# Turning the context of a Perceiver block by transposing DMAs instead of TensorE

## The chip, the cores and the metric

The kernel runs on one core of one Trainium2 chip, as one program. The metric is the device time of one execution in microseconds (us), the median of several runs. A profiled execution has the same kind of time, and beside it a span: from the first instruction of the core to the last.

## What is computed

Two batches (b = 0, 1) of 256 query tokens with 256 features attend to a context of 4096 tokens with 256 features; a second attention (hyperbolic distance) and a mixture of experts follow. Only the first attention and its inputs matter here:

```python
def xattn(query, key, value, w_q, w_k, w_v, w_o):     # 16 heads of 64
    q = (query @ w_q).reshape(B, Q, 16, 64).transpose(0, 2, 1, 3)
    k = (key @ w_k).reshape(B, 4096, 16, 64).transpose(0, 2, 1, 3)
    v = (value @ w_v).reshape(B, 4096, 16, 64).transpose(0, 2, 1, 3)
    attn = softmax(einsum('bhqd,bhkd->bhqk', q, k) * 64 ** -0.5)
    out = einsum('bhqk,bhkd->bhqd', attn, v)
    return out.transpose(0, 2, 1, 3).reshape(B, Q, 1024) @ w_o
x = x + xattn(layernorm(x), ctx, ctx, w_q, w_k, w_v, w_o)    # ctx: (2, 4096, 256) float32
x = x + attn(layernorm(x), ...)
x = x + ffn(layernorm(x), ...)
```

## The kernel before

**Steps and periods.** The first attention runs in 16 steps (STEPS), each for one pair of heads (hp) and one batch; ORDER lists them. A step has eight periods (q = 0 to 7), one for each chunk of 512 keys. In one period TensorE (PE) takes for the present step the shifts (L1431) and scores (L1443) of 512 keys, projects the values of the chunk (project_v, L1359) and multiplies the probabilities of the period before with values (L1486 to L1491). Beside that it computes for the next step the score blocks whose maximum is wanted (maxima, L1390) and projects the keys of the step after a chunk ahead (project_k, L1330). ScalarE (ACT) takes exponentials (L1677), high parts of probabilities (L1686), values and keys (L1643, L1637). VectorE (DVE) reduces the maxima (L1849), takes the high part of every fourth slot (split_p, L1877) and the low parts of values and keys (L1870, L1840). GpSimd (POOL) takes the low parts of the probabilities (L2048). Everything is in program order on each engine, with semaphores between them.

**High and low parts.** Each float32 factor is carried as two float16 arrays: the high part is the value cast, the low part is the value less the high part. A product takes three matmuls: high by high, high by low, low by high.

**The context.** Features must lie on the partitions for the projections, so each chunk of 512 tokens x 256 features is turned. `ctx_hi` and `ctx_lo` hold the turned parts of both batches. The raw chunks of batch 0 are loaded to `probs` and to the half of `k_p` that step 1 uses; those of batch 1 lie in the place of its own turned parts, one chunk further on.

**The stretch before step 0.** For i = 0 to 9 (the eight chunks of batch 0 and EARLY = 2 of batch 1) transposes_ctx(i) turns a chunk with eight float32 transposes on PE (L1288). ACT's context(i) reads the result from PSUM twice, once for the high part (L1660) and once for a float32 copy (L1662), for GpSimd cannot read PSUM. GpSimd subtracts the two for the low part (L2026). The next chunk's transposes wait for the second read, for they use the same two banks. Beside this PE projects the keys of step 0 (project_first_k, L1346), ACT and DVE take their high and low parts (L1637, L1840), and maxima of step 0 go through PE and DVE. At the end come the queries of step 1, its first chunk of keys, the greatest of the maxima (take_max) and the turned rows of it (max_rows); then step 0 begins.

**The rest of batch 1.** Step 1 was of batch 1, so its six other chunks (LATER_AT) are turned in the periods 0 to 5 of step 0: eight transposes on PE in two halves (transposes_later), two reads of 512 columns by ACT (L1667) and two by DVE (L1864).

**The queues.** All DMAs are issued from SyncE's queue (SP): x, the weights of steps 0 and 1, eight loads of batch 0, sixteen half chunks of batch 1, and then the weights for each step after its waits.

Of the kernel before, what the change touches and what calls it, by code (L numbers as in the profile page):

```python
# [59 lines left out]
TURNED = 2  # L60
EARLY = 2
PERIODS = SLOTS // 4
PAIRS_A_STEP = SLOTS // 2
LATER_AT = {q: q + EARLY for q in range(KCH - EARLY)}
# [37 lines left out]
def perceiver(nc, x, ctx, wq, wk, wv, wo, aq, ak, av, ao, gw, gb, w1, b1, w2, b2, out):  # L102
# [8 lines left out]
    with stack:  # L111

        ps = stack.enter_context(nc.psum_tensor("ps", [P, 8, 512], FP32))
        ctx_hi = sb("ctx_hi", [P, B, NC, TK], FP16)
        ctx_lo = sb("ctx_lo", [P, B, NC, TK], FP16)
# [6 lines left out]
        level = sb("level", [P, P], FP16)  # L122
        spare = sb("spare", [P, TK * 2])
# [34 lines left out]
        raw1 = [m[:, 1, :, :].rearrange("p c k -> p (c k)").bitcast(FP32)  # L158
                .rearrange("p (c u d) -> p c u d", c=NC, d=D) for m in (ctx_hi, ctx_lo)]
# [7 lines left out]
        copies = psums[:, :, :, :, :].rearrange("p b k h q -> p b k (h q)")  # L167


        hi32 = ctx_hi[:, :, :, :].rearrange("p b c k -> p (b c k)").bitcast(FP32)  # L170
        lo32 = ctx_lo[:, :, :, :].rearrange("p b c k -> p (b c k)").bitcast(FP32)
# [75 lines left out]
        s_tp = sem("s_tp")  # L247
        s_th = sem("s_th")
        s_tl = sem("s_tl")
        s_cx = sem("s_cx")  # L250
        s_ch = sem("s_ch")
        s_cl = sem("s_cl")
# [89 lines left out]
        def context_part(i):  # L342

            b, u = divmod(i, KCH)
            return b, u, slice(512 * u, 512 * (u + 1))

        def raw_tile(b, u, t):

            if b == 0:
                n = u // 2  # L350
                return stage[n // 2][:, n % 2, 4 * (u % 2) + t, :]
            if u == KCH - 1:
                return last_raw[:, t, :]
            return raw1[t // 2][:, t % 2, u + 1, :]
# [860 lines left out]
        def _(sp):  # L1215
# [18 lines left out]
            for u in range(KCH):  # L1234
                tiles = slice(4 * (u % 2), 4 * (u % 2) + 4)
                sp.dma_start(stage[u // 4][:, u // 2 % 2, tiles, :], chunks[0, u // 2, :, tiles, :]) \
                    .then_inc(s_ctx[u], 16)
                if u == 2:
                    load_wv(0, 0)
                    load_wqk(1, 0)  # L1240
            for u in range(KCH):
                for i in range(2):
                    to = last_raw[:, 2 * i:2 * i + 2, :] if u == KCH - 1 else raw1[i][:, :, u + 1, :]
                    first = 4 * (u % 2) + 2 * i
                    sp.dma_start(to, chunks[1, u // 2, :, first:first + 2, :]).then_inc(s_raw[u], 16)
            def load_experts(w):
                sp.dma_start(w_raw.rearrange("p (m n) -> p m n", n=F),
                             w.rearrange("e (c p) n -> p (e c) n", p=P)).then_inc(s_ew, 16)
# [22 lines left out]
            for n in range(STEPS):  # L1271
                step(n)
            tail_sp(sp)
# [3 lines left out]
        def _(pe):  # L1277
# [7 lines left out]

            def turn_context(b, u, c, bank):
                for t in range(CS):
                    mm = pe.transpose(ps[:, bank, t * P:(t + 1) * P],  # L1288
                                      raw_tile(b, u, t)[:, c * P:(c + 1) * P], ident[:, :])
                return mm  # L1290

            def transposes_ctx(i):

                b, u, _ = context_part(i)
                if b == 0:
                    pe.wait_ge(s_ctx[u], 16)
                else:
                    pe.wait_ge(s_raw[u], 32)
                at_least(pe, s_th, i)
                for c in range(NC):  # L1300
                    mm = turn_context(b, u, c, TURNED + c)
                mm.then_inc(s_tp, 1)

            def transposes_later(q, u, c):

                if c == 0:
                    pe.wait_ge(s_raw[u], 32)
                else:
                    pe.wait_ge(s_vl, q + 1)
                turn_context(1, u, c, (SIDE, PV)[c]).then_inc(s_cx, 1)  # L1310
# [10 lines left out]
            def project_k(j, n, par, b, bank):  # L1321
# [3 lines left out]
                if n == 1 and j >= EARLY:  # L1325
                    pe.wait_ge(s_cl, 2 * (j - EARLY) + 2)
                keys = slice(512 * j, 512 * (j + 1))
                for c in range(NC):
                    for i, (w, y) in enumerate(((wk_hi, ctx_hi), (wk_hi, ctx_lo), (wk_lo, ctx_hi))):
                        mm = pe.matmul(ps[:, bank, :], w[:, par, c, :], y[:, b, c, keys],  # L1330
                                       start=(c == 0 and i == 0), stop=(c == 1 and i == 2))
                mm.then_inc(s_k, 1)

            def project_first_k(j, bank):

                if j == 0:
                    pe.wait_ge(s_wkl, 1)
                keys = slice(512 * j, 512 * (j + 1))
                products = [(w, y, c) for w, y in ((wk_hi, ctx_hi), (wk_lo, ctx_hi), (wk_hi, ctx_lo))
                            for c in range(NC)]  # L1340
                for i, (w, y, c) in enumerate(products):
                    if i == 0:
                        pe.wait_ge(s_th, j + 1)
                    if i == 4:
                        pe.wait_ge(s_tl, j + 1)
                    mm = pe.matmul(ps[:, bank, :], w[:, 0, c, :], y[:, 0, c, keys],  # L1346
                                   start=(i == 0), stop=(i == 5))
                mm.then_inc(s_k, 1)

            def project_v(j, n, par, b, bank, halves=(0, 1)):  # L1350
# [3 lines left out]
                for t in [2 * half + i for half in halves for i in range(2)]:  # L1354
                    toks = slice((CS * j + t) * P, (CS * j + t + 1) * P)
                    k = 0
                    for c in range(NC):
                        for y, w in ((ctx_hi, wv_hi), (ctx_hi, wv_lo), (ctx_lo, wv_hi)):
                            mm = pe.matmul(ps[:, bank, t * P:(t + 1) * P], y[:, b, c, toks],  # L1359
# [5 lines left out]
            def maxima(u, n, par):  # L1365
# [13 lines left out]
                if n == 1 and t == 0:  # L1379
                    at_least(pe, s_cl, min(2 * j - 1, NC * len(LATER_AT)))  # L1380
# [74 lines left out]
            def values_bank_free(n, q):  # L1455
# [4 lines left out]
                if n == 0 and q - 1 in LATER_AT:  # L1460
                    pe.wait_ge(s_cl, 2 * q)
# [40 lines left out]
            def step(n):  # L1502
                par, b, first = n % 2, ORDER[n][1], n == 0
                for q in range(PERIODS):
# [18 lines left out]
                    if first and q in LATER_AT:  # L1523
                        transposes_later(q, LATER_AT[q], 0)
# [10 lines left out]
                    if first and q in LATER_AT:  # L1535
                        transposes_later(q, LATER_AT[q], 1)
# [49 lines left out]
            transposes_ctx(0)  # L1586
            transposes_x()
            project_first_k(0, PV)
            transposes_ctx(1)
            pe.wait_ge(s_xc, NC)  # L1590
            project_q(0, 0, 0)
            for j in range(2, KCH + 2):
                transposes_ctx(j)
                if j < KCH + 1:
                    at_least(pe, s_kl, j - 2)
                    project_first_k(j - 1, (PV, PK)[(j - 1) % 2])
                else:
                    pe.wait_ge(s_kl, KCH - 1)
                    project_q(1, 1, 1)
                maxima(2 * (j - 2), 0, 0)  # L1600
                maxima(2 * (j - 2) + 1, 0, 0)
            pe.wait_ge(s_kl, KCH)
            pe.wait_ge(s_tl, KCH + 1)
            project_k(0, 1, 1, 1, PK)
            max_rows(0)
            pe.wait_ge(s_tl, KCH + EARLY)
            pe.wait_ge(s_const, 4)
# [473 lines left out]
```

## Time and profile before

| | |
|---|---|
| median of 3 runs | 1123.02 us (1120.26 to 1123.82) |
| the profiled execution | 1124.97 us |
| its span | 1123.3 us |
| mean granted TensorE clock | 0.971 |
| step 0 begins (us from the span's start) | 50.3 |
| busy: PE, PEld, DVE, ACT, POOL | 94%, 70%, 72%, 71%, 61% |

PE is the matmul side of TensorE, PEld its weight loads. The profiled execution took 1.95 us more than the median of the three runs. A busy share is a mean over stretches with different limits, so each stretch has to be read by itself.

### The profile page before, as it was taken

What the parts mean: (1) busy time and instruction counts of PE and PEld (TensorE: products, weight loads), DVE (VectorE), ACT (ScalarE), POOL (GpSimd) and SP (SyncE); (2) the same over time, 40 slices, a digit from 0 to 9 for tenths busy, and PEclk for the clock granted to TensorE, in tenths of its full rate; (3) what the DMA queues carried; (4) which work ended last, traced back from release to release, by engine and by line L of the source; (5) the groups of instructions that cost most, each with busy time, mean ns of one, the idle gap of its engine ahead of it and who ended that gap; (6) DMA issues with size and microseconds to landing.
All of it is one profiled execution on the core that took longest, in us unless ns stands there. A gap on an engine that the chain in (4) does not pass through costs nothing.

```text
span 1123.3 us, 36747 instructions
## 1 busy us (share of the span) xinstructions
PE 1051.4 (94%) x15493; PEld 789.3 (70%) x15493; DVE 810.9 (72%) x1059; ACT 796.4 (71%) x1452; POOL 680.1 (61%) x614
## 2 busy tenths in 40 slices
PE   5899999999999999999999999999999999666688
PEld 3477777777777777777777777777777777543466
DVE  3887777777777777777777777777767759457442
ACT  4776776777777777777777777777776756798854
POOL 3665666666666666666666666676665556734233
PEclk9999999999999999999999999999999999787799
DMA  9100000000000000000000000003000010000000
GB/s 329 51 2 16 7 17 7 17 6 17 7 16 7 17 7 17 7 16 8 17 7 16 8 16 7 16 8 119 7 2 7 28 52 3 2 1 1 1 1 20
DMA packets 27381, 25.45 MB, mean 23 GB/s; under 512 B 1850, under 2 KB 25938, under 8 KB 27218
## 3 DMA queue, kind: packets, MB, share of 16 engines
q1 hardware_dynamic: 27218, 23.10, 6.5%
q8 instruction: 124, 2.03, 0.7%
q14 instruction: 39, 0.32, 0.1%
HBM read 22.57 MB, written 0.52 MB: 21 GB/s over the span
## 4 chain that ended last, share of the span: by engine, by line
PE 81%; DVE 8%; issue 4%; ACT 4%; POOL 2%; DMA 1%; SPq 0%; ACTq 0%; POOLq 0%; DVEq 0%
PE ps L1359 15%; PE ps L1330 14%; PE ps L1443 13%; PE ps L1390 6%; PE ps L1491 5%; PE ps L1486 5%; PE ps L1489 5%; PE ps L1431 4%; PE ps L759 2%; PE ps L719 2%; POOL psums L2048 2%; PE ps L1422 1%; PE ps L1316 1%; DVE m_part L1849 1%; PE ps L535 1%
## 5 line engine op out<-in xcount | busy, mean ns | idle before, releaser
L2048 POOL TENSOR_TENSOR psums<-probs 128x512 f16<-128x512 f32 x512 | 590.1, 1172 | 317.5 <-ACT probs L1686 264.2
L1677 ACT ACTIVATE probs<-ps 128x512 f32<-128x512 f32 x512 | 279.7, 600 | 199.2 <-PE ps L1443 198.3
L1849 DVE TENSOR_REDUCE m_part<-ps 128x2 f32<-128x1024 f32 x256 | 313.2, 1224 | 142.8 <-PE ps L1390 142.7
L1686 ACT ACTIVATE probs<-probs 128x512 f16<-128x512 f32 x384 | 242.1, 632 | 0.3
L1443 PE MATMUL ps<-q_hi,k_p 64*128 64x256 f16 x2048 | 211.1, 269 | 0.0
L1486 PE MATMUL ps<-v_sb,probs 128*128 128x65 f16 x2048 | 205.9, 193 | 4.5 <-POOL psums L2048 4.5
L1489 PE MATMUL ps<-v_sb,probs 128*128 128x64 f16 x2048 | 205.8, 192 | 0.0
L1491 PE MATMUL ps<-v_sb,psums 128*128 128x65 f16 x2048 | 205.4, 194 | 0.0
L1486 PEld LDWEIGHTS ps<-v_sb,probs 128*128 128x128 f16 x2048 | 188.4, 98 | 19.0 <-POOL psums L2048 6.1
L1489 PEld LDWEIGHTS ps<-v_sb,probs 128*128 128x128 f16 x2048 | 188.0, 97 | 15.6
L1491 PEld LDWEIGHTS ps<-v_sb,psums 128*128 128x128 f16 x2048 | 188.2, 97 | 0.0
L1359 PE MATMUL ps<-wv_hi,ctx_hi 128*128 128x128 f16 x1024 | 180.5, 221 | 1.6 <-DVE v_sb L1870 1.6
L1359 PE MATMUL ps<-wv_lo,ctx_hi 128*128 128x128 f16 x1024 | 179.2, 220 | 0.0
L1359 PE MATMUL ps<-wv_hi,ctx_lo 128*128 128x128 f16 x1024 | 179.2, 220 | 0.0
L1877 DVE CAST probs<-probs 128x512 f16<-128x512 f32 x128 | 147.7, 1154 | 1.6 <-ACT probs L1677 1.4
L1443 PE MATMUL ps<-q_lo,k_p 64*128 64x256 f16 x1024 | 142.8, 269 | 0.0
L1359 PEld LDWEIGHTS ps<-wv_hi,ctx_hi 128*128 128x128 f16 x1024 | 100.2, 98 | 40.2 <-issue 38.3
L1443 PEld LDWEIGHTS ps<-q_hi,k_p 64*128 64x128 f16 x2048 | 106.1, 94 | 19.5
L1840 DVE TENSOR_TENSOR k_p<-ps,k_p 128x512 f16<-128x512 f32 x128 | 88.5, 691 | 33.3 <-ACT k_p L1637 33.3
L1390 PE MATMUL ps<-k_p,q_hi 64*128 64x512 f16 x512 | 99.0, 380 | 13.2 <-DVE m_part L1849 7.9
L1359 PEld LDWEIGHTS ps<-wv_lo,ctx_hi 128*128 128x128 f16 x1024 | 100.6, 98 | 0.1
L1359 PEld LDWEIGHTS ps<-wv_hi,ctx_lo 128*128 128x128 f16 x1024 | 100.4, 98 | 0.0
(246 smaller groups left out, 1704.4 us busy)
## 6 DMA issues: line engine op xcount, KB each, us to landing
ctx_hi<-in_L_ffn_W_dram SPq DMA_DIRECT2D x2, 2048.0 KB, 9.7
wqk_raw<-in_L_xattn_w_q_dram SPq DMA_DIRECT2D x16, 128.0 KB, 2.3
wqk_raw<-in_L_xattn_w_k_dram SPq DMA_DIRECT2D x16, 128.0 KB, 2.5
probs<-in_ctx_dram SPq DMA_DIRECT2D x4, 512.0 KB, 7.4
wv_raw<-in_L_xattn_w_v_dram SPq DMA_DIRECT2D x16, 128.0 KB, 2.5
k_p<-in_ctx_dram SPq DMA_DIRECT2D x4, 512.0 KB, 9.2
wo_raw<-in_L_xattn_w_o_dram SPq DMA_DIRECT2D x16, 128.0 KB, 2.1
ctx_hi<-in_ctx_dram SPq DMA_DIRECT2D x7, 256.0 KB, 7.0
```

Of the source, the lines that this page charges most:

```text
L1330: mm = pe.matmul(ps[:, bank, :], w[:, par, c, :], y[:, b, c, keys], start=(c == 0 and i == 0), stop=(c == 1 and i == 2))
L1359: mm = pe.matmul(ps[:, bank, t * P:(t + 1) * P], y[:, b, c, toks], w[:, par, c, :], start=(k == 0), stop=(k == 5))
L1390: mm = pe.matmul(ps[:, bank + 1 - h, :], q_hi[rows, n % 3, t * P:(t + 1) * P], k_p[rows, par, 0, 512 * j:512 * (j + 1)], start=True, stop= ...
L1443: mm = pe.matmul(ps[:, score_bank(n, pair, h), cols], k_p[rows, par, k_part, keys], q_part[rows, n % 3, :], start=False, stop=(i == 2), sk ...
L1486: pe.matmul(out, p_hi[:, s % NP, h, queries], value[:, XD:2 * XD + 1], start=(s == 0 and h == 0 and t == 0), stop=False, skip_group_check= ...
L1489: pe.matmul(ps[:, ACC, at:at + XD], p_hi[:, s % NP, h, queries], value[:, 0:XD], start=False, stop=False, skip_group_check=True)
L1491: mm = pe.matmul(out, p_lo[:, s % NP, h, queries], value[:, XD:2 * XD + 1], start=False, stop=(s == SLOTS - 1), skip_group_check=True)
L1677: nc.scalar.activation(p_raw[:, s:s + 2, h, :], ps[:, score_bank(n, pair, h), :].rearrange("p (k q) -> p k q", k=2), ACT.Exp, scale=XSCALE ...
L1686: nc.scalar.activation(p_hi[:, s % NP, :, :], p_raw[:, s % NX, :, :], ACT.Copy) \
L1849: nc.vector.tensor_reduce(m_part[:, j, t, :], ps[:, bank:bank + 2, :], AX.X, ALU.max) \
L1877: nc.vector.tensor_copy(p_hi[:, s % NP, :, :].rearrange("p h q -> p (h q)"), p_raw[:, s % NX, :, :].rearrange("p h q -> p (h q)")) \
L2048: nc.gpsimd.tensor_tensor(p_lo[:, s % NP, :, :].rearrange("p h q -> p (h q)"), p_raw[:, s % NX, :, :].rearrange("p h q -> p (h q)"), p_hi[ ...
```

## The change

1. The raw chunks are split where they lie, tokens on the partitions: ACT casts 128x1024 for the high part (split_context_high) and GpSimd takes raw less high for the low part (split_context_low), both into `nat`, a ring of NAT = 8 buffers. No PE transposes, no copies through PSUM.
2. Each part is turned by a transposing DMA of 128x1024 float16 (256 KB) within SBUF, from the SP queue (turn_context). A chunk needs two. `ctx_hi` and `ctx_lo` are laid out by chunk.
3. Batch 0 is now loaded from ACT's queue, batch 1 from SP's between the turning DMAs.
4. For the keys of step 0, the low part is made in PSUM: a further matmul adds minus the identity times the high part (subtract_high), and ACT casts what is left (take_low_k). DVE's subtraction of before is gone there. ACT casts up to LEAD = 4 chunks ahead.
5. Steps 0 and 1 are both of batch 0 (head pairs 0 and 1), so batch 1 is first needed by step 2's keys (FIRST1 = 2), from period 7 of step 0. Its chunks 2 to 7 are split in halves of 128x512, one in each of the first twelve periods: on ACT ahead of the period's exponentials, on DVE between the two maxima.
6. GpSimd's constants for the tail come at the beginning and not after the chunks.

```diff
-ORDER = tuple((i // 2, i % 2) for i in range(STEPS - 6)) + tuple(
+ORDER = ((0, 0), (1, 0), (0, 1), (1, 1)) + tuple((i // 2, i % 2) for i in range(4, STEPS - 6)) + tuple(
     (hp, b) for b in range(B) for hp in range(HP - 3, HP))
+FIRST1 = 2
-TURNED = 2
-LATER_AT = {q: q + EARLY for q in range(KCH - EARLY)}
+SPLIT_AT = {g: (KCH + EARLY + g // 2, g % 2) for g in range(2 * (KCH - EARLY))}
+NAT = 8
+LEAD = 4
+        def split_context_high(act, i, halves=(0, 1)):
+            b, u = divmod(i, KCH)
+            if b == 0:
+                act.wait_ge(s_ctx[u], 16)
+            else:
+                act.wait_ge(s_raw[u], 32)
+            if i >= NAT:
+                act.wait_ge(s_dh[i % NAT], 16)
+            parts = raw_parts(i)
+            for raw, tiles in [parts[h] for h in halves if h < len(parts)]:
+                last = nc.scalar.activation(nat_part(i, 0, tiles), raw, ACT.Copy)
...
+        def split_context_low(eng, ops, i, halves=(0, 1)):
...
+            for raw, tiles in [parts[h] for h in halves if h < len(parts)]:
+                last = ops.tensor_tensor(nat_part(i, 1, tiles), raw, nat_part(i, 0, tiles), ALU.subtract)
...
+            def turn_context(i, low):
...
+                sp.dma_start((ctx_hi, ctx_lo)[low][:, b, u, :, :].rearrange("p c (t k) -> p (c t) k", t=CS),
+                             nat[:, i % NAT, low, :], transpose=True).then_inc((s_dh, s_dl)[low][i % NAT], 16)
+            turn_context(0, 0)
+            for u in range(1, KCH + 1):
+                if u < KCH:
+                    turn_context(u, 0)
+                turn_context(u - 1, 1)
+                if u - 1 in (3, 5):
+                    load_context((u - 4) // 2)
+            for u in range(2, KCH):
+                load_context(u)
+                if u in (3, 5):
+                    turn_context(KCH + u // 4, 0)
+                    turn_context(KCH + u // 4, 1)
...
             for n in range(STEPS):
+                if n == 2:
+                    for u in range(EARLY, KCH - 3):
+                        turn_context(KCH + u, 0)
+                        turn_context(KCH + u, 1)
                 step(n)
+                if n == 2:
+                    for u in range(KCH - 3, KCH):
+                        turn_context(KCH + u, 0)
+                        turn_context(KCH + u, 1)
...
             pe.wait_ge(s_const, 3)
-            transposes_ctx(0)
             transposes_x()
-            project_first_k(0, PV)
-            transposes_ctx(1)
+            project_first_k(0, 0)
             pe.wait_ge(s_xc, NC)
             project_q(0, 0, 0)
-            for j in range(2, KCH + 2):
-                transposes_ctx(j)
...
+            project_first_k(0, 1)
+            pe.wait_ge(s_const, 5)
+            for j in range(KCH):
+                if j + 1 < KCH:
+                    for part in range(2):
+                        project_first_k(j + 1, part)
+                subtract_high(j)
+                maxima(2 * j, 0, 0)
+                maxima(2 * j + 1, 0, 0)
...
             split_k(0, 0)
-            context(0)
+            split_context_high(act, 0)
+            split_context_high(act, 1)
...
+            split_context_high(act, 2)
             take_q(0)
+            split_context_high(act, 3)
+            for j in range(KCH):
+                take_k(j, 0, 0, (PV, PK)[j % 2])
+                if j >= 1:
+                    take_low_k(j - 1)
+                if j + LEAD < KCH:
+                    split_context_high(act, j + LEAD)
```

## Rows read from the trace of the kernel before

**Rows 1.** The chain that ended last, to period 5 of step 0: start us, us, what.
```profile
2.34 6.08 DMA probs<-in_ctx_dram
...
26.18 1.04 PE ps L1288 x8
27.24 1.02 ACT ctx_hi L1660
28.26 0.93 ACT psums L1662
...
42.38 0.61 PE ps L1346 x2
...
80.56 0.66 PE ps L1443 x12
...
88.00 0.66 PE ps L1443 x12
```
**Rows 2.** TensorE's timeline: first and fifteenth maxima of step 0, first instruction of step 0.
```profile
22.25 0.61 PE L1390 MATMUL ps<-k_p,q_hi 64*128 64x512 f16 x4
...
45.35 0.39 PE L1390 MATMUL ps<-k_p,q_hi 64*128 64x512 f16 x2
...
50.31 0.39 PE L1390 MATMUL ps<-k_p,q_hi 64*128 64x512 f16 x2 [0.67 <-ACT m_row L1654]
```
**Rows 3.** Groups by line and form, 0 to 50.3 us: xcount | busy us, mean ns.
```profile
L2026 POOL TENSOR_TENSOR ctx_lo<-psums,ctx_hi 128x1024 f16<-128x1024 f32 x10 | 21.3, 2129 | 25.7 <-ACT psums L1662 25.7
L1849 DVE TENSOR_REDUCE m_part<-ps 128x2 f32<-128x1024 f32 x16 | 19.3, 1217 | 4.0 <-PE ps L1390 4.0
...
L1637 ACT ACTIVATE k_p<-ps 128x512 f16<-128x512 f32 x9 | 5.4, 602 | 3.8 <-PE ps L1346 2.4 <-PE ps L1330 1.5
```
**Rows 4.** The chain in two periods of step 2, as in rows 1.
```profile
195.95 0.65 PE ps L1443 x12
...
202.59 0.66 PE ps L1443 x12
```
**Rows 5.** The timeline of one period of step 1: start us, us, engine, line, tiles.
```profile
139.90 2.27 POOL L2048 TENSOR_TENSOR psums<-probs 128x512 f16<-128x512 f32 x2
140.74 1.23 DVE L1849 TENSOR_REDUCE m_part<-ps 128x2 f32<-128x1024 f32 x1 [0.58 <-PE ps L1390]
...
141.61 1.57 ACT L1677 ACTIVATE probs<-ps 128x512 f32<-128x512 f32 x3 [1.65 <-PE ps L1443]
...
142.70 1.23 DVE L1849 TENSOR_REDUCE m_part<-ps 128x2 f32<-128x1024 f32 x1 [0.73 <-PE ps L1390]
...
143.98 0.39 PE L1330 MATMUL ps<-ctx_hi,wk_hi 128*128 128x512 f16 x1
```
**Rows 6.** Two lines over the whole span: ns, shortest/median/longest.
```profile
L1686 ACT ACTIVATE probs<-probs x384: 612/624/677, 53.1 to 962.8; 128x512 f16<-128x512 f32 x192
...
L1817 DVE SCALAR_TENSOR_TENSOR wv_lo<-wv_raw,wv_hi x16: 411/411/1293, 33.6 to 865.4; 128x256 f16<-128x256 f32 x16
```
**Rows 7.** The DMA view: SP's queue (packets, MB, share of 16 engines); issues (KB, us to landing).
```profile
q1 hardware_dynamic: 27218, 23.10, 6.5%
...
ctx_hi<-in_ctx_dram SPq DMA_DIRECT2D x7, 256.0 KB, 7.0
...
out_dram<-x_sb SPq DMA_DIRECT2D x2, 256.0 KB, 2.7
```
**Rows 8.** The timeline of SP's queue: one issue.
```profile
0.81 0.43 SPq L1231 DMA_DIRECT2D x_sb<-in_x_dram  x1
```
**Rows 9.** Windows: length, busy of PE, PEld, DVE, ACT, POOL, granted clock, DMA share, GB/s.
```profile
16.00:18.00 2.00, 2.00 (x9) 1.91 (x9) 0.69 (x1) 0.89 (x2) 0.00 (x0) 0.50 1.03 377
...
22.00:24.00 2.00, 2.00 (x16) 1.20 (x15) 1.31 (x2) 1.21 (x3) 1.29 (x1) 1.00 1.10 348
```
**Rows 10.** VectorE's timeline in period 6 of step 0 and at the start of period 7.
```profile
102.47 0.22 DVE L993 TENSOR_REDUCE vecs<-ident 128x1 f32<-128x4 f32 x2
...
105.02 1.22 DVE L1849 TENSOR_REDUCE m_part<-ps 128x2 f32<-128x1024 f32 x1
```

More of the change, by code:

```diff
@@ L246, in perceiver @@
         s_xc = sem("s_xc")
-        s_tp = sem("s_tp")
         s_th = sem("s_th")
         s_tl = sem("s_tl")
-        s_cx = sem("s_cx")
-        s_ch = sem("s_ch")
-        s_cl = sem("s_cl")
+        s_dh = [sem(f"s_dh{i}") for i in range(NAT)]
+        s_dl = [sem(f"s_dl{i}") for i in range(NAT)]
+        s_kn = sem("s_kn")
+        s_t2 = sem("s_t2")
+        s_t3 = sem("s_t3")
         s_wkh = sem("s_wkh")
@@ L1329, in project_k, with project_first_k, subtract_high @@
                     for i, (w, y) in enumerate(((wk_hi, ctx_hi), (wk_hi, ctx_lo), (wk_lo, ctx_hi))):
-                        mm = pe.matmul(ps[:, bank, :], w[:, par, c, :], y[:, b, c, keys],
+                        mm = pe.matmul(ps[:, bank, :], w[:, par, c, :], y[:, b, j, c, :],
                                        start=(c == 0 and i == 0), stop=(c == 1 and i == 2))
                 mm.then_inc(s_k, 1)
[L1334 to L1347, printed above, removed]
+            def project_first_k(j, part):
+                keys, bank = slice(512 * j, 512 * (j + 1)), (PV, PK)[j % 2]
+                if part == 0:
+                    at_least(pe, s_kl, j - 1)
+                    if j == 0:
+                        pe.wait_ge(s_wkl, 1)
+                    pe.wait_ge(s_dh[j], 16)
+                    for w in (wk_hi, wk_lo):
+                        for c in range(NC):
+                            pe.matmul(ps[:, bank, :], w[:, 0, c, :], ctx_hi[:, 0, j, c, :],
+                                      start=(w is wk_hi and c == 0), stop=False)
+                    return
+                pe.wait_ge(s_dl[j], 16)
+                for c in range(NC):
+                    mm = pe.matmul(ps[:, bank, :], wk_hi[:, 0, c, :], ctx_lo[:, 0, j, c, :],
+                                   start=False, stop=(c == NC - 1))
                 mm.then_inc(s_k, 1)
+            def subtract_high(j):
+                pe.wait_ge(s_kh, j + 1)
+                pe.matmul(ps[:, (PV, PK)[j % 2], :], minus[:, :], k_p[:, 0, 0, 512 * j:512 * (j + 1)],
+                          start=False, stop=True, skip_group_check=True).then_inc(s_kn, 1)
             def project_v(j, n, par, b, bank, halves=(0, 1)):
@@ L1707, in step @@
                         take_v(0, n + 1, MX)
-                    if first and q in LATER_AT:
-                        context_later(LATER_AT[q], 0)
                     if n == DONE0 and q in TURN_IN:
@@ L1714, in step @@
                     high(n, s + 3)
-                    if first and q in LATER_AT:
-                        context_later(LATER_AT[q], 1)
                     if q == OT_IN and not first:
@@ L1986, in _ @@
             normalised(0, slice(0, NT))
-            for j in range(1, KCH + 2):
-                if j >= 2:
-                    maxima(2 * (j - 2), 0)
-                if j == 5:
+            take_q(0)
+            for j in range(KCH):
+                maxima(2 * j, 0)
+                if j == 3:
                     split_v(0, 0)
-                if j == 6:
+                if j == 4:
                     split_k(1, 1)
-                if j < KCH + 1:
-                    take_k(j - 1, 0, 0, (PV, PK)[(j - 1) % 2])
-                if j == 1:
-                    take_q(0)
-                if j == KCH + 1:
-                    take_q(1)
-                if j >= 2:
-                    maxima(2 * (j - 2) + 1, 0)
+                maxima(2 * j + 1, 0)
+            take_q(1)
             take_max(0)
```

182 lines of the change are left out of this document (80 added, 102 removed).

## The prediction

> **What bounds the kernel now.** I read the page first: PE is busy for 94% of the span and every other engine for 61 to 72%. The chain that ended last then says where that mean hides something. It has two sorts of stretches.
>
> *From step 0 on* the chain is TensorE alone. Two periods of step 2 begin 202.59 - 195.95 = 6.64 us apart [rows 4], with nothing but matmuls between. In step 0 the same two marks stand 88.00 - 80.56 = 7.44 us apart [rows 1]: 0.80 more in each of the six periods that turn a chunk of batch 1.
>
> *Before step 0* the chain goes round between engines: eight transposes 1.04, ACT's cast 1.02, ACT's copy 0.93 [rows 1], then the next transposes, since the two banks are free only then. Maxima of step 0 show the pace: the first at 22.25, the fifteenth at 45.35, seven chunks later [rows 2], so 23.10 / 7 = 3.30 us a chunk. Step 0 begins at 50.31. No engine's own work for a chunk fills that: DVE has two reductions of 1.22, POOL 2.13 [rows 3].
>
> So 50.3 us are set by a loop over three engines, 6 x 0.80 us by PE, and the remaining 1068 us the change leaves as they are, but for what it adds to steps 0 and 1.
>
> **The price on which it turns: c, the time of one transposing DMA when they queue.** The trace before has none. Sixteen stand one behind another on SP's queue before step 0, each of 256 KB. From below: the loads moved 348 GB/s between 22 and 24 us [rows 9], so 256 KB take 0.75 us; nothing lets a transposing transfer be cheaper than a plain one of its size. From above: if it moves in runs of 256 bytes (128 float16 of one partition), it has 1024 packets. The queue's 27218 packets took 6.5% of 16 engines' 1123.3 us, which is 0.043 us each on one engine [rows 7]; 1024 x 0.043 / 16 = 2.75 us. Those packets were 849 bytes in the mean, so part of 0.043 is bytes and 2.75 is a real upper end for this way of moving. I take 1.5, near the geometric middle of 0.75 and 2.75 (1.44), since neither end is nearer in kind. A single one lands later than c: 256 KB alone took 2.7 us to land, in a full queue 7.0 [rows 7], so I add 2.0 behind the last.
>
> The Trainium skill speaks on both sides. "DMA: Bandwidth & Descriptors", Latency and other measured facts, gives 261 GB/s for a DMA transpose: an estimate of 1.0 us for 256 KB, with which the pace below would not be the DMA's, and the sum would come to 1113. "VectorE: DVE Perf Modes", The three transpose paths and the rules behind it, speaks against the change: 1309 ns by DMA for 128x128 where TensorE needs 390, and TensorE where a result in PSUM will do. Paid for each of the eight blocks of a transfer that would be an estimate of 10.5 us. No trace here shows either; the second is the third rival below.
>
> **Part by part, before step 0.**
> - *Front.* The first raw chunk landed at 8.42, issued at 2.34 behind three other loads [rows 1]. From ACT's queue it goes out at once but shares the DMA engines with x. ACT's cast of 1.02 then ends at 9.2 in my reckoning, between 8.1 (landed by 7.1) and 9.4 (landed as before). POOL's part follows 2.13 later.
> - *Turning.* From 9.2 the SP queue turns both parts of eight chunks: 16 x 1.5 = 24.0. Between them stand four loads of batch 1, 256 KB each, at 0.75: 3.0. The last lands 2.0 later: 9.2 + 24.0 + 3.0 + 2.0 = 38.2. POOL's parts (2.13 a chunk [rows 3]) come faster than 2c = 3.0 and are hidden behind it; so are ACT's casts.
> - *Other loops.* DVE: 2 x 1.22 = 2.44 a chunk. ACT: two takes of 0.60 and a cast of 1.02, 2.22. The loop of ACT and PE: take_k 0.60, take_low_k 0.60, PE's next six products at 0.22 (512 columns at the full clock [rows 9] are 512 / 2.4 GHz = 0.213), 1.3, and three hand-overs that I put at some 0.07 each: 2.7. subtract_high costs PE 0.22 a chunk, in that loop's shade. All are under 3.0. Were the DMAs free (c = 0.75), 2.7 would be the pace: first maxima at 19.5 (turning of two chunks and the queries' products, part of it at half clock), seven chunks on at 38.4, and 50.31 - 45.35 = 4.96 for the end as before: 43.4.
> - *End.* In the trace before, the last product of the eighth chunk begins at 42.38 and step 0 at 50.31, 7.9 us later [rows 1, 2]. The same work follows the last landing now: 38.2 + 7.9 = 46.1, against 50.3. **Gain 4.2**; with c = 0.75 it is 6.9, with c = 2.75 (58.2 + 7.9 = 66.1) a loss of 15.8.
> - *Clock.* PE's granted clock was 0.50 between 16 and 18 us (1.2 GHz), 1.00 later [rows 9]. Now PE has no early transposes and may be at 1.2 GHz some microseconds longer. Six products at twice 0.22 add 1.3 to a chunk, once or twice; the DMAs' pace hides most of that. At nothing; up to 2.6 without that cover.
>
> **Steps 0 and 1.**
> - *Transposes gone:* six periods fall from 7.44 to 6.64. **Gain 4.8**.
> - *ACT's half casts* take 0.62 (the same shape, float32 to float16 in SBUF [rows 6]). They stand where ACT was idle for 1.65 us for want of scores [rows 5]. Nothing.
> - *DVE's half subtractions*, twelve, stand between the two maxima. The first reduction ends at 141.97, POOL is busy until 142.17, and the second reduction begins at 142.70 and ends at 143.93, 0.05 us before PE's project_k, which waits for it [rows 5]. An operation of DVE with two inputs in SBUF took 0.411 for 256 columns and 1.293 once, beside POOL [rows 6]: it can be held until POOL is done. So it runs from 142.17 for some 0.7 (my estimate for 512 columns, between 0.411 and twice that) to 142.87, and pushes PE by 0.17 us. Later periods inherit some of the shift from POOL too. **Loss 1.2** (twelve times 0.1); from 0 to 12 x (1.293 - 0.411) = 10.6.
> - *Period 7 of step 0.* DVE's row vectors, from 102.47, held its first reduction of the period up until 105.02 [rows 10]; PE waited. A half subtraction of 0.7 now stands right behind it. **Loss 0.7**, from 0 to 0.9.
> - *Keys of step 2* need chunk 0 of batch 1 turned by period 7 of step 0, and the last chunk, split in period 3 of step 1, by period 6. That leaves three periods, 20 us, for two transfers. Hidden up to c of about 6. The weights of step 2 go out behind twelve loads and four more transfers, and are first used some twelve periods (80 us) after step 0 begins. Hidden too.
>
> **Sum.** -4.2 - 4.8 + 1.2 + 0.7 = -7.1 us. Against the profiled execution, 1124.97, that is 1117.9; it stood 1.95 above the median of the three runs, so for the median 1123.0 - 7.1 = 1115.9: **1116.0 us**.
>
> **Rivals.**
> 1. *The DMAs are no bound* (c near 0.75 to 1.2). For it: 348 GB/s are there and the batch's loads are over early. Then 43.4 instead of 46.1, and 1123.0 - 6.9 - 2.9 = 1113; with no loss in DVE 1111. Chance 0.27.
> 2. *The transposing DMAs become the bound: slower.* One mechanism: sixteen in a row on one queue. Step 0 begins at 9.2 + 16c + 3.0 + 2.0 + 7.9 = 22.1 + 16c. The kernel is even with before when that is 50.3 + 2.9 = 53.2, so at c = 1.94, inside my bounds. With c = 2.75 it is 66.1 and the kernel takes 1123.0 + 15.8 - 2.9 = 1136. For it: small packets; against it: source and destination are both on the core. Chance 0.20 for c from 2.1 to 3.
> 3. *Issued block by block.* If each of eight 128x128 blocks costs what one DMA costs SP to issue, 0.43 us [rows 8], c is 3.4, step 0 begins at 76.5, and the kernel takes 1123.0 + 26.2 - 2.9 = 1146. The rule in "VectorE: DVE Perf Modes" quoted above is of this kind, and its block price is higher still. Chance 0.12.
> 4. *DVE's half subtractions stall PE in all twelve periods* by 0.88: +9.4 on my sum, 1125. DVE's work in a period would be 5.6 of 6.64, so it could catch up; chance 0.06.
> The forecast itself (c from 1.2 to 1.8): 0.35.
>
> **How the numbers follow.** A difference under 0.3% (3.4 us) can't be told from none here. Faster: the forecast but for its slower edge, and rival 1, 0.60. Within 0.3%: c near 1.94, or rival 4, 0.08. Slower: rivals 2 and 3 and a little of 4, 0.32. The range reaches from 1108 (rival 1 with a front a few us earlier) to 1140, which takes in rival 2 with c up to 3. Left out are rival 3 and a little below. The forecast's own range is 1111 to 1121.
>
> **What would show it.** In the profile after: the distance between the landings of two transposing DMAs before step 0 (1.5); step 0's first scores at 46.1; maxima 3.0 us a chunk apart, with waits of PE's project_first_k for a DMA; periods of 6.64 to 6.8 in step 0; DVE's half subtractions at 0.7, or 1.2 and more if held by POOL; no wait of ACT's for batch 1's raw chunks. Wrong would be: any c beyond 1.94, SP's issue time of a transposing DMA far over 0.43, or a PE that stands at 1.2 GHz for the whole stretch.

## The result, and the profile after

The changed kernel takes 1128.45 us in the median of 8 runs (1126.14 to 1129.99), the kernel before 1121.33 (8 runs, 1120.11 to 1123.82). The ratio is 1.0056, with a 95% interval from 1.0042 to 1.0070. It is slower by 0.6%, some 6 to 7 us. Forecast were 1116 and a gain, with a chance of 0.32 for a loss; 1128.45 lies inside the stated range of 1108 to 1140, on the side that had the smaller chance. The two profiled executions took 1124.97 (before) and 1126.14 us (after), so their traces differ by 1.2 us only.

The chain that ended last, of the profiled execution after (start us, us, what), answers to [rows 1]:

```profile
1.86 11.26 DMA wqk_raw<-in_L_xattn_w_k_dram
...
22.03 1.09 ACT xnT L1798 x2
23.12 0.95 ACT spare L373
...
25.36 3.33 DMA ctx_lo<-spare
...
41.73 4.79 DMA ctx_lo<-spare
...
49.38 0.43 PE ps L1396 x2
...
57.92 0.66 PE ps L1497 x12
...
64.57 0.66 PE ps L1497 x12
...
114.69 0.66 PE ps L1497 x12
```

The chain before step 0 no longer goes round PE, ACT and PSUM. For its first 25 us it is a load of weights, the layernorm of x (the kernel before had both done by 10 us) and ACT's third cast. Step 0's scores begin at 57.9, 7.0 us later than before. Then the periods of step 0 are 6.64 us, as those of later steps were [rows 4], and no longer 7.44 [rows 1]. At the first scores of step 1 (114.69; before it was 113.37) 5.7 of the 7.0 us are back.

The timeline after, before step 0 (start us, us, engine, line, tiles):

```profile
13.15 0.42 ACT L1665 ACTIVATE wk_hi<-wqk_raw 128x256 f16<-128x256 f32 x1 [3.57 <-DMA wqk_raw<-in_L_xattn_w_k_dram]
13.47 1.99 ACT L373 ACTIVATE spare<-probs 128x1024 f16<-128x1024 f32 x2
14.54 3.47 SPq L1295 DMA_TRANSPOSE ctx_hi<-spare  x2
14.60 4.20 POOL L389 TENSOR_TENSOR spare<-probs,spare 128x1024 f16<-128x1024 f32 x2 [7.83 <-ACT spare L373]
14.74 1.99 DVE L1851 TENSOR_TENSOR rstd<-rstd,newton 128x4 f32<-128x4 f32 x1
16.77 3.14 DVE L1853 TENSOR_SCALAR xn<-x_sb,mv,rstd 128x256 f32<-128x256 f32 x4
18.05 1.31 SPq L1295 DMA_TRANSPOSE ctx_lo<-spare  x1
...
24.09 1.23 SPq L1295 DMA_TRANSPOSE ctx_hi<-spare  x1
...
26.77 1.30 SPq L1295 DMA_TRANSPOSE ctx_hi<-spare  x1
28.11 1.33 SPq L1295 DMA_TRANSPOSE ctx_lo<-spare  x1
29.49 1.34 SPq L1295 DMA_TRANSPOSE ctx_hi<-spare  x1
29.49 0.61 PE L1444 MATMUL ps<-k_p,q_hi 64*128 64x512 f16 x4
...
51.77 0.39 PE L1444 MATMUL ps<-k_p,q_hi 64*128 64x512 f16 x2 [0.80 <-DVE m_part L1895]
...
57.32 0.39 PE L1444 MATMUL ps<-k_p,q_hi 64*128 64x512 f16 x2 [1.36 <-DVE k_p L1886]
```

Three marks answer to [rows 2]. The first maxima come at 29.49 and not at 22.25: 7.2 us lost at the front. The fifteenth come at 51.77, so 3.18 us a chunk against 3.30: 0.8 won. From there to step 0 it is 5.55 us and not 4.96: 0.6 lost. Together 7.0.

The front, the work before the first maxima, reads so. The key weights went out at 1.86 and were cast only at 13.15, because ACT's queue had sent 4 MB of raw context onto the same DMA engines. ACT's first casts stand behind that. When they are done, GpSimd's first two subtractions hold DVE up: an operation on four columns took 1.99 us, and four of 0.35 each took 3.14. So x is normalised at 19.9. ACT waits for its turned rows until 22.03, casts the third chunk at 23.00, and SP's queue has nothing to turn between 19.4 and 24.1.

The turning DMA itself is as I had reckoned, or better. The DMA view after (SP's queue: packets, MB, share of 16 engines), a window with the DMA engines' share and GB/s at the end, and the view of the last turning DMA of batch 0:

```profile
q1 hardware_dynamic: 58066, 27.30, 10.0%
```
```profile
26.00:30.00 4.00, 1.94 (x11) 0.42 (x8) 0.33 (x2) 2.80 (x5) 3.44 (x3) 1.00 0.99 190
```
```profile
L1295 SPq DMA_TRANSPOSE ctx_lo<-spare x1: 1309/1309/1309, 44.5 to 44.5; - x1
...
DMA to landing us min/median/max: 3.2/3.2/3.2
```

In a row they are issued some 1.37 us apart (26.77, 28.11, 29.49) and fill the engines: a busy share of 0.99, at 190 GB/s. The last one of batch 0 goes out at 44.5 and lands at 47.7.

### The profile page after: what moved, and what is told of

Read it like the earlier page. It is cut to its first block, busy times and chain, and to the rows that moved or that the text cites. A ratio compares the mean times of both kernels' runs of the same rounds, so it can differ in the third digit from the quotient of the medians.

```text
span 1124.4 us, 36557 instructions
## 1 busy us (share of the span) xinstructions
PE 1038.0 (92%) x15373; PEld 774.9 (69%) x15373; DVE 809.8 (72%) x1052; ACT 791.8 (70%) x1452; POOL 681.7 (61%) x617
## 3 DMA queue, kind: packets, MB, share of 16 engines
q1 hardware_dynamic: 58066, 27.30, 10.0%
q10 hardware_dynamic: 1152, 4.19, 1.0%
## 4 chain that ended last, share of the span: by engine, by line
PE 80%; DVE 8%; issue 4%; ACT 3%; POOL 2%; DMA 2%; SPq 0%; ACTq 0%; POOLq 0%; DVEq 0%
PE ps L1415 15%; PE ps L1377 14%; PE ps L1497 13%; PE ps L1444 6%; PE ps L1543 5%; PE ps L1538 5%; PE ps L1541 5%; PE ps L1485 4%; PE ps L796 2%; PE ps L756 2%; POOL psums L2081 2%; PE ps L1476 1%; PE ps L1362 1%; PE ps L572 1%; DMA wqk_raw<-in_L_xattn_w_k_dram 1%
## 5 line engine op out<-in xcount | busy, mean ns | idle before, releaser
L1415 PEld LDWEIGHTS ps<-wv_hi,ctx_hi 128*128 128x128 f16 x1024 | 100.1, 98 | 40.8 <-issue 38.9
L1886 DVE TENSOR_TENSOR k_p<-ps,k_p 128x512 f16<-128x512 f32 x120 | 83.0, 691 | 28.2 <-ACT k_p L1681 28.2
## 6 DMA issues: line engine op xcount, KB each, us to landing
ctx_hi<-in_L_ffn_W_dram SPq DMA_DIRECT2D x2, 2048.0 KB, 10.1
```

The costliest lines, as they stand in the source:

```text
L1415: mm = pe.matmul(ps[:, bank, t * P:(t + 1) * P], y[:, b, j, c, toks], w[:, par, c, :], start=(k == 0), stop=(k == 5))
```

## The experiments

Each starts from the changed kernel unless it says otherwise. The ratio is to the kernel before. The granted clock in brackets is TensorE's, 1.0 for 2.4 GHz and 0.5 for 1.2 GHz.

**Loads from SP's queue again.**

```diff
             load_wqk(0, 0)
-            load_wv(0, 0)
-            load_wqk(1, ORDER[1][0])
+            for u in range(KCH):
+                tiles = slice(4 * (u % 2), 4 * (u % 2) + 4)
+                sp.dma_start(stage[u // 4][:, u // 2 % 2, tiles, :], chunks[0, u // 2, :, tiles, :]) \
+                    .then_inc(s_ctx[u], 16)
+                if u == 2:
+                    load_wv(0, 0)
+                    load_wqk(1, ORDER[1][0])
...
-            for u in range(KCH):
-                tiles = slice(4 * (u % 2), 4 * (u % 2) + 4)
-                act.dma_start(stage[u // 4][:, u // 2 % 2, tiles, :], chunks[0, u // 2, :, tiles, :]) \
-                    .then_inc(s_ctx[u], 16)
```

> The changed kernel, but batch 0's eight raw loads go out from SP's queue again, in the order of the kernel before (x, first weights, three chunks, further weights, five chunks). Theory A (the front is late because 4 MB from ACT's queue share the DMA engines with x and the key weights, which landed at 13.1 us): the cast of the key weights comes back from 13.15 to about 6.7 us, the layernorm is out of GpSimd's way, the first maxima come at 23 to 24 us instead of 29.5 and step 0 begins near 51 instead of 57.3: about 1122 us. Theory B (the sum of all bytes on the 16 engines sets the stretch, raw and turned parts one behind another): the first turning DMAs now queue behind the raw loads, land at 17 us or later, and step 0 begins no earlier than 55: 1126 us or more.

Measured: 1126.85 us, ratio 1.0053 (1.0032 to 1.0074), not to be told from the changed kernel. The weights were cast at 6.92 and x was normalised by 10.1, as theory A says. But the first maxima came at 26.9, not at 23 to 24, and step 0 began at 58.9. A line of DVE's timeline, one of SP's, and the view of the first turning DMA alone:

```profile
8.70 1.38 DVE L1854 TENSOR_SCALAR xn<-x_sb,mv,rstd 128x256 f32<-128x256 f32 x4
9.70 9.14 SPq L1300 DMA_TRANSPOSE ctx_hi<-spare  x2
```
```profile
L1300 SPq DMA_TRANSPOSE ctx_hi<-spare x1: 5382/5382/5382, 9.7 to 9.7; - x1
...
DMA to landing us min/median/max: 10.4/10.4/10.4
```

The first turning DMA held the queue for 5.4 us instead of 1.3 and landed after 10.4: it waits behind the raw loads, which keep all engines busy until about 18 us. So theory A names a real wait, but with the weights cast 6.2 us earlier the last turning DMA of batch 0 landed only 1.7 earlier, at 46.0. That much of B holds. The 1.7 and 1.6 more were lost behind that landing, where the chain has no DMA in it, but matmuls that took 3.2 us longer than the changed kernel's: the granted clock from there to step 0 was 0.74 in the mean, and 1.00 in the changed kernel.

**DVE normalises first.**

```diff
             variance(0, slice(0, NT))
+            normalised(0, slice(0, NT))
             split_k(0, 0)
-            normalised(0, slice(0, NT))
```

> The changed kernel, but DVE normalises x before it takes the low part of the key weights, for which it had to wait until 13.6 us. Theory A2 (it is the port shared by DVE and GpSimd, held by GpSimd's first two subtractions from 14.6 to 18.8, that makes the normalised rows late, at 19.9, and ACT's third cast with them, at 23.0): normalised by 12 us with four operations of 0.35 each, third cast at 17 to 18, step 0 about 4 to 5 us earlier: 1123 to 1124 us. Theory B (sum of bytes): the gap on SP's queue closes, but the pace after it drops, and under 2 us are won: 1127.

Measured: 1124.97 us, ratio 1.0027 (1.0014 to 1.0039), some 3 us better than the changed kernel. Timeline of this kernel, DVE and ACT:

```profile
10.43 0.16 DVE L1851 TENSOR_TENSOR rstd<-rstd,newton 128x4 f32<-128x4 f32 x1
10.63 1.38 DVE L1853 TENSOR_SCALAR xn<-x_sb,mv,rstd 128x256 f32<-128x256 f32 x4
...
13.71 0.42 ACT L1665 ACTIVATE wk_hi<-wqk_raw 128x256 f16<-128x256 f32 x1 [4.19 <-DMA wqk_raw<-in_L_xattn_w_k_dram]
...
16.89 1.05 ACT L373 ACTIVATE spare<-probs 128x1024 f16<-128x1024 f32 x1
```

The same operation took 0.16 us out of GpSimd's way, and the third cast came at 16.89 instead of 23.00. Theory A2 is shown. The first maxima came at 25.46, 4.0 earlier; but the fifteenth at 51.57, where they had been (3.73 us a chunk), and in this profiled execution step 0 began no earlier (58.8). The DMAs explain only a part: the last turning DMA landed at 45.3, 2.4 before the changed kernel's, so 1.6 of the 4.0 were given back there. The rest went behind it, at the lower clock. Windows of this kernel, then one of the changed kernel from its last landing to step 0 (the third number from the end is the granted clock):

```profile
43.40:50.20 6.80, 6.11 (x18) 1.43 (x18) 2.36 (x3) 3.10 (x6) 3.02 (x3) 0.50 0.93 212
53.60:57.00 3.40, 3.40 (x10) 1.47 (x9) 1.75 (x4) 0.38 (x1) 0.00 (x0) 0.50 1.53 220
```
```profile
47.70:57.30 9.60, 6.30 (x32) 2.65 (x29) 8.12 (x9) 5.29 (x12) 2.27 (x2) 1.00 0.95 240
```

The six products for step 1's keys took 2.57 us here and 1.31 there. The profiled execution (1127.26) is also the slowest of this kernel's eleven. So it doesn't contradict the 3 us won in the median; that the others spent less time at 1.2 GHz is likely and not shown.

**Both repairs, loads staggered.** DVE as above; SP issues x, the first weights and four raw chunks, ACT the other four between its casts.

```diff
             load_wqk(0, 0)
+            for u in range(4):
+                tiles = slice(4 * (u % 2), 4 * (u % 2) + 4)
+                sp.dma_start(stage[u // 4][:, u // 2 % 2, tiles, :], chunks[0, u // 2, :, tiles, :]) \
+                    .then_inc(s_ctx[u], 16)
...
-            for u in range(KCH):
...
+            def load_first(units):
+                for u in units:
...
             split_context_high(act, 0)
+            load_first((4, 5))
             split_context_high(act, 1)
+            load_first((6, 7))
```

> Both repairs: DVE normalises first, SP issues four raw chunks behind x and the first weights, and ACT issues the other four between its first casts. Theory A: key weights cast by 7, first maxima near 22, step 0 at 49 to 50, and with the 5.7 us won in step 0 the kernel is at 1120 or below, so no slower than the kernel before. Theory B: step 0 at 53 or later, 1124.

Measured: 1131.57 us, ratio 1.0091 (1.0075 to 1.0108): the worst of all, against theory A and beyond B. The first maxima came at 30.1 and step 0 began at 62.0. Its first turning DMA, issued at 9.9 with raw loads before and behind it on two queues, took the longest:

```profile
L1299 SPq DMA_TRANSPOSE ctx_hi<-spare x1: 6471/6471/6471, 9.9 to 9.9; - x1
...
DMA to landing us min/median/max: 13.7/13.7/13.7
```

**Batch 1 later.** Nothing of batch 1 is loaded, split or turned before step 0.

```diff
-EARLY = 2
-SPLIT_AT = {g: (KCH + EARLY + g // 2, g % 2) for g in range(2 * (KCH - EARLY))}
+EARLY = 0
+SPLIT_AT = {g: (KCH + g, (0, 1)) for g in range(3)}
+SPLIT_AT.update({3 + i: (KCH + 3 + i // 2, (i % 2,)) for i in range(10)})
...
                 turn_context(u - 1, 1)
-                if u - 1 in (3, 5):
-                    load_context((u - 4) // 2)
-            for u in range(2, KCH):
+            for u in range(KCH):
                 load_context(u)
...
-                if j in (5, 6):
-                    split_context_high(act, KCH + j - 5)
```

> The changed kernel, but nothing of batch 1 is loaded, split or turned before step 0: its loads come behind the last turning DMA of batch 0, its first three chunks are split whole in periods 0 to 2 of step 0. Takes 1 MB of loads, two casts on ACT and four subtractions on GpSimd out of the stretch; adds a second half subtraction on DVE in three periods. Theory B (the DMA engines' sum is the pace behind the front): the waits of PE for the turned low parts of chunks 4 and 6 go, step 0 begins 3 us earlier, 1125.5. Theory A (all is lost at the front): the pace of 3.18 us a chunk stays and the time is the changed kernel's, 1128.

Measured: 1123.97 us, ratio 1.0018 (1.0008 to 1.0028), 4 us better than the changed kernel. The first maxima stood where they were (29.84), the fifteenth came at 48.02: 2.60 us a chunk. The DMA engines are full of turning alone (the last two numbers are their share and GB/s). The chain of the same stretch has no DMA in it:

```profile
30.00:38.00 8.00, 6.69 (x33) 1.95 (x29) 6.85 (x6) 6.14 (x11) 6.17 (x4) 1.00 1.01 190
```
```profile
34.77 0.53 PE ps L1392 x2
...
35.32 0.60 ACT k_p L1677
35.92 0.50 ACT k_p L1699
...
36.46 1.04 PE ps L1387 x4
37.49 0.46 PE ps L1392 x2
```

Two transfers at 1.37 are 2.74 us a chunk, and the loop of PE and ACT takes 37.49 - 34.77 = 2.72, the 2.7 of the prediction: the two bounds are level here, and a faster turning alone would win nothing. The early part of batch 1 cost 4.1 us of pace. That it is its four loads, and not the casts and subtractions that went with them, SP's queue shows: in the changed kernel the eight turning DMAs from 30.9 to 44.5 (with batch 1 later from 31.2 to 40.8) are seven steps of 1.37 and 4.0 us more, all of it around the two pairs of loads. I had put 3.0.

**Front and later together.**

> Two earlier edits together: DVE normalises x first, and batch 1 is loaded and turned behind batch 0. Theory B (behind the front, the pace is that of the sum of bytes on the DMA engines; a repaired front is given back only as long as batch 1's loads stand between the turning DMAs): the first maxima come at 25.5 us as with the first edit alone, the pace is 2.6 to 2.75 us a chunk (two turning DMAs at 1.37), step 0 begins near 50 to 51 and the time is 1120 us, 1 or 2 below the kernel before. Theory A (front and pace are separate losses and add fully, with no bound behind): 55.4 less 4.4 is 51.0, nearly the same time. Theory C (a repaired front is given back by the DMAs in any case): first maxima at 25.5, but a pace above 3 us and a step 0 at 54 or later, 1124 us.

Measured: 1121.47 us, ratio 0.9994 (0.9982 to 1.0005). First maxima at 25.32, a pace of (45.48 - 25.32) / 7 = 2.88, step 0 at 52.7: pace, place and time lie between B's and C's. The last turning DMA landed at 41.5. With both edits the kernel is level with the kernel before, though its step 0 still begins 2.4 us later. In the ratios the two edits add: 0.29% for the first alone, 0.38% for the second alone, 0.62% together. So in the median the repaired front is kept.

**Low parts of the keys on DVE.** On top of both edits:

```diff
-                subtract_high(j)
...
-                if j >= 1:
-                    take_low_k(j - 1)
...
-            take_low_k(KCH - 1)
...
             for j in range(KCH):
+                take_k(j, 0, 0, (PV, PK)[j % 2])
                 maxima(2 * j, 0)
```

> The kernel with both edits, but the low part of the keys of step 0 is taken by DVE from PSUM as before, not by minus the identity on PE and a cast on ACT. If the DMAs set the pace (2.74 us a chunk), DVE's sum of 2 x 1.22 + 0.69 = 3.13 us now does: some 0.4 us a chunk more, 3 us in all, about 1123. If PE and ACT's loop set it, the time falls or stays, 1120.

Measured: 1123.61 us, ratio 1.0019 (1.0002 to 1.0035). The number is that of the first expectation, but the profiled execution shows only 0.8 us of its 3: the fifteenth maxima came at 46.23 instead of 45.48, a pace of 2.93. Step 0 even began 0.9 earlier, at 51.8, for the last kernel's trace had a stretch at 1.2 GHz from 46.9 to 50.3 (granted clock 0.51) and this one has none before step 0. The median is 2 us above the last kernel's, but the two intervals meet (1.0002 and 1.0005). Inconclusive.

**Batch 0 by TensorE, batch 1 by DMA.** The stretch before step 0 is that of the kernel before, without chunks of batch 1; the order of steps, the split in periods and the turning DMAs for batch 1 are those of the kernel with batch 1 later.

```diff
+            transposes_ctx(0)
             transposes_x()
-            project_first_k(0, 0)
+            project_first_k(0, PV)
+            transposes_ctx(1)
...
+            for j in range(2, KCH + 2):
+                if j < KCH:
+                    transposes_ctx(j)
+                if j < KCH + 1:
+                    at_least(pe, s_kl, j - 2)
+                    project_first_k(j - 1, (PV, PK)[(j - 1) % 2])
```

> Batch 0 is turned by TensorE, copied and split as in the kernel before, with all loads on SP's queue in its order; steps 0 and 1 are of batch 0, and the eight chunks of batch 1 are split and turned by DMA in the periods of these steps. My account (the stretch before step 0 lost 7.0 us, steps 0 and 1 won 5.7, and the two are independent): step 0 begins at 49 to 50.3, since the last two rounds have no chunk of batch 1 to turn, and the time is 1121.4 - 5.7 = 1115.7 or up to 1 less. Rival (the half casts and half subtractions need the slack that a late start left, or the turning DMAs in steps disturb the loads of weights): step 0 takes 60 us or more, 1119 or above.

Measured: 1119.7 us, ratio 0.9973 (0.9960 to 0.9986), faster than the kernel before by 3 us, but not by 5.7 (of which, as said further down, 1.6 were a fall of the clock in the trace of before). Step 0 began at 49.1, as expected, and then ran longer. The chain of this kernel:

```profile
48.68 0.38 ACT m_row L1692
49.06 1.03 ACT spare L370 x2
50.12 1.28 ACT L1709
...
55.51 0.70 DVE k_p L1873
...
56.35 0.39 PE ps L1435 x2
...
57.07 1.28 PE ps L1488 x12
```

Two casts of batch 1 stand between max_rows and the first exponentials, with ACT's table load (1.28) behind them. PE waits for keys until 56.35 and then runs twelve score matmuls in 1.28 us instead of 0.66: at half clock (granted clock 0.50 from 56.7 to 60.1).

**Two chunks ahead.** On top of the last: chunks 0 and 1 of batch 1 are split by ACT and GpSimd and turned in their idle time before step 0, the others in halves, one a period, as in the changed kernel.

```diff
-EARLY = 0
...
+EARLY = 2
+SPLIT_AT = {g: (KCH + EARLY + g // 2, (g % 2,)) for g in range(2 * (KCH - EARLY))}
...
+            for u in range(EARLY):
+                turn_context(KCH + u, 0)
+                turn_context(KCH + u, 1)
...
+            for i in range(KCH, KCH + EARLY):
+                split_context_high(act, i)
             take_q(1)
```

> The kernel that turns batch 0 by TensorE and batch 1 by DMA, but two chunks of batch 1 are split and turned in the idle time of ACT and GpSimd just before step 0, and the others in halves, one a period, as in the changed kernel. Before this edit two casts of ACT stood ahead of the first exponentials, PE waited for the keys 2.1 us in the first period and then ran for 4 us at half clock: step 0 took 58.4 us from max_rows to max_rows against 56.8 in the changed kernel. Theory (the doubled casts and subtractions of periods 0 to 2 cost that): 56.8 again, 1.6 us gained, so about 5.5 to 6 us below the kernel before. Rival (the half clock comes from PE's sparse work before step 0 and stays): nothing gained, 3 us below as now.

Measured: 1117.75 us, ratio 0.9963 (0.9947 to 0.9978), the fastest of all kernels here, some 4 to 5 us below the kernel before and 10 below the changed one. The chain:

```profile
55.71 0.66 PE ps L1490 x12
...
62.35 0.65 PE ps L1490 x12
```

From max_rows to max_rows step 0 takes 103.4 - 47.5 = 55.9 us, against 58.4, and its granted clock is 1.00 from 50 to 60: the trace bears the theory out, and the rival's half clock is not there. The gain in the medians is 2 us, less than forecast, and the intervals of the two ratios overlap.

## Why the prediction was wrong

**The price c was right, in part by luck.** 1.5 us had been taken for a turning DMA in a row, as the middle of two bounds that lie apart by a factor of 3.7; 1.37 was measured. The packets are what the upper bound assumed: (58066 + 1152 on ACT's queue - 27218 [rows 7]) / 32 = 1000 for each transfer. Each took about 1.37 x 16 / 1000 = 0.022 us of an engine, half of what the mean packet of before took. None of the rivals, which all turned on c or on DVE in the periods, was the cause, and the break-even at c = 1.94 was never passed. The Trainium skill's 261 GB/s for a DMA transpose ("DMA: Bandwidth & Descriptors", Latency and other measured facts) was not reached, 190 were; its 1309 ns for one 128x128 block ("VectorE: DVE Perf Modes", The three transpose paths) are not paid per block, for eight blocks landed in 3.2 us.

**The step that failed is "Front" and "Turning": that turning begins at 9.2 and goes on without a gap.** The last turning DMA of batch 0 was to land at 38.2. It was issued at 44.5 and landed 3.2 later, at 47.7. Of these 9.5 us, 5.3 are the late beginning (14.5), 4.7 the empty queue between 19.4 and 24.1, -2.1 the better c (16 x 0.13), and 1.6 are what is left: batch 1's loads, which cost 4.1 and not 3.0, and the landing. The end behind it took 9.6 and not 7.9. From the last product (49.38) to step 0 it was 7.9, as in the trace before; the other 1.7 are that PE and ACT still had the seventh chunk in hand when the eighth landed. 46.1 + 9.5 + 1.7 is the measured 57.3.

Three things stood behind this step, and I had asked about none of them. I moved eight loads to a second queue and priced only what they deliver, not what they delay: the weights, cast at 13.15 instead of 6.67. I did not follow DVE's order, in which the normalisation stands behind the key weights, into the time in which GpSimd subtracts; there was a row for what that costs (0.411 and 1.293, [rows 6]), used for the steps only. And I let turning start at 9.2 at its full rate while 5.3 MB of loads, at 348 GB/s [rows 9], fill the engines until 17 or 18 us.

For the landings the last is the one that decides. With loads and turning in one sum the estimate would have been (two turning DMAs are out when the loads end at 18) 18 + 14 x 1.37 + 4.1 + 3.2 = 44.5 for the last landing, and without batch 1's loads 40.4. The kernels whose front was repaired stand 0.8 to 1.5 us behind these sums: 45.3 and 46.0 with the loads, 41.5 without. With the 7.9 behind it, 44.5 gives 52.4 for step 0, later than before even with a perfect front.

The clock, put at nothing, cost the changed kernel's trace nothing behind the last landing, but the repaired ones something. The traces, from the last landing to step 0:

| kernel | last landing | step 0 begins | between | granted clock between |
|---|---|---|---|---|
| changed | 47.7 | 57.3 | 9.6 | 1.00 |
| loads from SP's queue | 46.0 | 58.9 | 12.9 | 0.74 |
| DVE normalises first | 45.3 | 58.8 | 13.5 | 0.69 |
| both, staggered | 49.3 | 62.0 | 12.7 | 0.73 |
| batch 1 later | 44.1 | 55.2 | 11.1 | 0.85 |
| front and later | 41.5 | 52.7 | 11.2 | 0.85 |
| low parts on DVE | 41.1 | 51.8 | 10.7 | 1.00 |

The changed kernel's own trace has its 3.4 us at 1.2 GHz from 38.9 on, ahead of the last landing. So the clock is not what made it slow, but it took up to some 4 us from the repairs in their traces. (With the low parts on DVE the 10.7 at full clock are DVE's, busy for 10.1 of them.)

One reading of the kernel before was wrong without harm. "No engine's own work for a chunk fills" the 3.30 us left out DVE's low part of the keys: a window from 25.4 to 45.4 has DVE busy for 18.5 of 20.0 us, so DVE was nearly a bound too. The change takes that operation from DVE.

**The steps.** The 4.8 us for the transposes gone came (4.7): periods of 6.64. The loss of 0.7 in period 7 of step 0 came too. There DVE's half subtraction was held for 1.36 us, and PE's keys waited for the maxima behind it (VectorE's and PE's timelines after):

```profile
108.45 1.36 DVE L389 TENSOR_TENSOR spare<-ctx_lo,spare 128x512 f16<-128x512 f32 x1
```
```profile
111.01 0.39 PE L1377 MATMUL ps<-ctx_hi,wk_hi 128*128 128x512 f16 x1 [0.49 <-DVE m_part L1895]
```

PE's matmul before that starts at 110.30 and the keys at 111.01, where 0.10 lies between the two in the period before: 0.6 lost. The loss of 1.2 in the other periods did not come: there the half subtractions took 0.68 to 0.91 us, and the periods of step 1 are the same before and after to 0.01. GpSimd was out of the way more often than [rows 5] had suggested. The marks show 5.7 us won in step 0, where 2.9 had been forecast for both steps. But 1.6 of it belong to this one profiled execution of the kernel before, whose clock fell in period 7 of step 0 (windows; the third number from the end is the granted clock):

```profile
102.10:109.00 6.90, 4.99 (x66) 3.99 (x62) 5.59 (x23) 2.58 (x5) 2.58 (x4) 0.84 0.19 57
109.00:116.00 7.00, 7.00 (x109) 5.10 (x107) 3.46 (x4) 4.44 (x9) 3.16 (x3) 0.91 0.01 2
```

Twenty-four value products took 2.60 us there and 1.45 elsewhere, six key products 1.78 and not 1.34: 1.6 us. So the steps won 4.1, 1.2 more than forecast. The profiled execution after had no fall there, but one later:

```profile
821.00:827.00 6.00, 4.11 (x31) 2.78 (x32) 4.00 (x6) 2.80 (x6) 2.74 (x3) 0.74 0.00 0
```

The same products took 2.05 and 2.35 us there, 1.6 more than in the trace before.

**How much of the 6 to 7 us is shown.** Before step 0 7.0 were lost and in the steps 4.1 won: 2.9 us, and 4.5 with the fall at 824. The remaining 2 us or so no trace shows. The two traces differ by 1.2 us only, since the fall in step 0 slowed the one of before, which is also 1.9 us slower behind 900 us, where the change edits nothing (granted clock 0.87 before, 0.89 after). The profiled execution of before lies 3.6 us above the median of the eight runs and above the slowest of them; the one of after is the fastest of its eight, 2.3 below the median. That falls of the clock come and go from one execution to the next, and make the scatter of 3.5 to 8 us within each kernel's runs, is likely, but no run here shows it: there is one trace of each kernel. The forecast was also set off from 1123.0, the median of three runs; eight gave 1121.33.

**What stays open.** What makes up the last 2 us or so of the median's loss; why the clock fell behind the last landing in five of the traces and not in two; and whether the low parts by the negative identity win or lose anything.

## What to carry to other kernels

When a transfer replaces work of an engine, add its bytes to everything else that the DMA engines move in that stretch, at their measured rates, before asking about its latency: two queues share one set of engines. A load moved to another queue has a price in what it now overtakes; list the small loads behind it and who waits for each. When a repair seems to be given back, look at the granted clock behind it before blaming the bound that you have in mind. A turning DMA pays where the DMA engines are idle and an engine is the bound (here the steps), and not in the stretch in which the inputs come in: taking it only in the steps made the kernels that beat the one before.

## What the runs showed of the hardware

- A DMA that turns 128x1024 float16 within SBUF held SP's queue for 1.23 to 1.34 us in a row of such DMAs and landed 3.1 to 3.5 us after issue; the pace was 1.37 us, 190 GB/s with the engines' share at 1.0, against 348 for plain loads of the context [rows 9].
- Beside raw loads of 4 MB the first of them landed after 4.7 us (issued at 14.5, changed kernel), 10.4 (at 9.7, loads on the same queue) and 13.7 (at 9.9, loads on both queues), and its issue alone took 5.4 and 6.5 us in the last two, so that everything behind it on SP's queue waited too.
- Weights of 128 KB issued at 1.86 landed at 13.1 with 4 MB issued from ACT's queue between 0.8 and 5.3, and at 5.4 with the same loads behind them on SP's queue.
- An operation of DVE on 128x4 with both inputs in SBUF took 1.99 us instead of 0.16 (DVE normalises first) while GpSimd subtracted 128x1024, and one of 128x256 with one input and two pointers was slowed as well (four in 3.14 us instead of 1.38). This agrees with the Trainium skill ("SBUF — State Buffer", Who interferes with whom), by which the two engines share a port pair that one of them holds for a whole instruction.
